# Products that nobody reads on TensorE ahead of three layer norms of a four-layer graph network

## What is computed

```python
xn = _layernorm(x, axis=-1)
x = x + gnn(xn, edge_index, ...) + mix(xn[None], ...)[0]
x = x + ffn(_layernorm(x, axis=-1)[None], ...)[0]
```

```python
def _layernorm(x, axis=-1, eps=1e-05):
    m = jnp.mean(x, axis=axis, keepdims=True)
    v = jnp.var(x, axis=axis, keepdims=True)
    return (x - m) / jnp.sqrt(v + eps)
```

## Time and profile before

| what | us |
|---|---|
| median of 3 runs | 7233.67 |
| lowest and highest run | 7231.20, 7253.52 |
| the profiled execution | 7236.89 |
| its span, first to last instruction | 7235.2 |
| TensorE busy | 5270.6 (73%) |
| VectorE busy | 4311.6 (60%) |
| GpSimd busy | 3786.5 (52%) |
| mean granted clock of TensorE | 0.825 |

### The profile page before, as it was taken

How to read it: one execution, slowest core, us unless ns; L and a number is a source line. 1 busy time by engine, 2 the same in 40 slices (tenths; PEclk the granted TensorE clock), 3 DMA queues, 4 the chain that set the end, 5 groups by cost and what they waited for, 6 DMA issues and landing times. The chain is left out here.

```text
span 7235.2 us, 73313 instructions
## 1 busy us (share of the span) xinstructions
PE 5270.6 (73%) x20758; PEld 3340.7 (46%) x20758; DVE 4311.6 (60%) x12546; ACT 938.7 (13%) x2436; POOL 3786.5 (52%) x3736
## 2 busy tenths in 40 slices
PE   4451767729767778868787885867778888886798
PEld 3241733327634333347685542544443224334687
DVE  8961977772355555552499887766634774445311
ACT  1010011112200010022201231211010001000222
POOL 2776077705477557715303774037744774774233
PEclk9975789759898865669898997888889998565899
DMA  2110543427633333337542334023335774333565
GB/s 62 49 33 12 174 109 105 105 68 189 152 104 105 82 89 105 106 66 191 149 152 64 103 101 100 9 71 100 102 68 147 210 209 116 105 106 68 183 190 172
DMA packets 345016, 801.97 MB, mean 111 GB/s; under 512 B 96963, under 2 KB 196807, under 8 KB 331845
## 3 DMA queue, kind: packets, MB, share of 16 engines
q0 software_dynamic: 202752, 491.35, 26.5%
q1 hardware_dynamic: 141872, 305.94, 13.5%
HBM read 722.42 MB, written 77.80 MB: 111 GB/s over the span
## 5 line engine op out<-in xcount | busy, mean ns | idle before, releaser
L2129 PE MATMUL bank<-arena 128*125 128x256 f32 (+3 forms) x5824 | 2545.2, 539 | 855.3 <-DMA arena<-TAB,arena 349.5
L2112 POOL DMA_INDIRECT arena<-TAB,arena x2080 | 1988.3, 956 | 1308.5 <-DMA TAB<-arena 658.0
L2129 PEld LDWEIGHTS bank<-arena 128*125 128x125 f32 x5824 | 1110.3, 230 | 2241.8 <-DVE arena L2152 675.9
L2173 DVE TENSOR_TENSOR arena<-bank,arena 125x256 f32 (+3 forms) x2912 | 1354.3, 465 | 1147.6 <-PE bank L2129 1108.5
L2112 POOL DMA_INDIRECT arena<-TABa,arena x832 | 831.2, 999 | 847.3 <-ACTq L141 575.1
L2152 DVE TENSOR_SCALAR arena<-arena 128x125 f32<-128x125 f32 x2080 | 617.1, 297 | 62.8 <-PE bank L2129 50.9
L1732 POOL DMA_INDIRECT REC<-arena x400 | 449.5, 1124 | 231.0 <-issue 120.4
L1336 POOL DMA_INDIRECT SUM<-arena x192 | 307.4, 1601 | 465.3 <-DVE arena L1546 402.9
L341 PE MATMUL bank<-arena 128*125 128x256 f32 (+4 forms) x1600 | 439.5, 421 | 90.2 <-DVE arena L2268 24.0
L1381 PE MATMUL bank<-arena 128*128 128x256 f32 x2048 | 465.9, 384 | 6.5 <-DVE arena L1534 6.1
L1395 PE MATMUL bank<-arena 128*128 128x256 f32 x2048 | 466.2, 384 | 0.0
(11 more groups left out here) (501 smaller groups left out, 5496.8 us busy)
## 6 DMA issues: line engine op xcount, KB each, us to landing
arena<-L_ffn_pack SPq DMA_DIRECT2D x32, 2054.0 KB, 9.0
arena<-L_ffn_pack SPq DMA_DIRECT2D x64, 1026.0 KB, 5.6
arena<-TAB,arena POOLq DMA_INDIRECT x2080, 2.8
arena<-SLR SPq DMA_DIRECT2D x52, 512.0 KB, 3.7
arena<-DLR SPq DMA_DIRECT2D x52, 512.0 KB, 4.7
arena<-TABa,arena POOLq DMA_INDIRECT x832, 2.8
arena<-L_ffn_b SPq DMA_DIRECT2D x96, 128.0 KB, 5.6
arena<-LROW SPq DMA_DIRECT2D x20, 610.4 KB
```

Of the source, the lines that this page charges most:

```text
L2112: e.indirect_dma_start(out=m.G[k % RING][:, 0:m.width], out_offset=None, in_=m.table[:, :], in_offset=bass.IndirectOffsetOnAxis(ap=eidx[:, ...
L2129: e.matmul(ps[0:P, 0:m.full], m.S[k % SRING], m.G[k % RING], start=True, stop=True).then_inc(*put("pass_p", m.g, "summed", k))
L2173: e.tensor_tensor(o, banks.of(m.g, "added", k)[0:P, 0:m.full], o, ALU.add).then_inc(*put("pass_v", m.g, "added", k))
```

## The change

A new function, `unread_pe`, is called at three places of TensorE's program, each time right ahead of `norm_pe`. It takes a bank, and for each step of a list waits for that step and then issues 28 matrix products of bf16: the first 128 of J128's 256 columns read as bf16 are the stationary operand, all 256 are the moving one. All go to the same 256 columns of one bank, each starting anew, and nothing reads them. At layers 0 and 2 the list is the five adds of the join and then the first half's variance; at layer 3 it is tiles 4, 9, 14, 19 and 24 of the last sum and then the first half's variance. Nothing else changes.

```diff
--- before.py
+++ after.py
@@ -305,6 +305,19 @@
         turn_act(e, g, XT, AFTER)
 
     gateW, gateb = at(PV + 496, 2, 8, p=128), [at(PV + 512 + 8 * i, 8) for i in range(2)]
+
+    def unread_pe(e, g, steps):
+
+
+        v = J128.bitcast(BF16)
+        ps, before = banks.take(g, "unread")
+        if before:
+            e.wait_ge(*of(*before))
+        for step in steps:
+            e.wait_ge(*of(*step))
+            for i in range(28):
+                ins = e.matmul(ps[:, 0:256], v[:, 0:128], v, start=True, stop=True)
+        ins.then_inc(*put("unread_p", g, "unread"))
 
     def norm_pe(e, g, gate=None):
 
@@ -3026,6 +3039,7 @@
         pass_pe(e, gats[0].run, [l0_queries_pe(e)], LOW)
         r = rest(e, r + 1)
         banks.clear()
+        unread_pe(e, "n0f", [("a0", "joined", i) for i in range(5)] + [("n0f", "var", 0)])
         norm_pe(e, "n0f", gate_of(moes[0]))
         r = rest(e, r + 1)
         banks.clear()
@@ -3052,6 +3066,7 @@
         pass_pe(e, gats[1].run, l2_mix_pe(e), LOW3)
         r = rest(e, r + 1)
         banks.clear()
+        unread_pe(e, "n2f", [("a2", "joined", i) for i in range(5)] + [("n2f", "var", 0)])
         norm_pe(e, "n2f", ("f2", f2wr, "half_p", "gate"))
         r = rest(e, r + 1)
         banks.clear()
@@ -3060,6 +3075,7 @@
         r = rest(e, r + 1)
         banks.clear()
         l3_gnn_pe(e)
+        unread_pe(e, "n3f", [("d3", "out", t) for t in range(4, T, 5)] + [("n3f", "var", 0)])
         norm_pe(e, "n3f", gate_of(moes[2]))
         r = rest(e, r + 1)
         banks.clear()
```

## The result

The changed kernel took 7253.48 us, the median of 17 runs (7236.75 to 7436.58), beside 7234.97 for the kernel before in 17 runs; the ratio is 1.0018, with an interval of 1.001 to 1.0026. The 7436.58 is a single run at a mean granted clock of 0.747 instead of some 0.83, and the ratio leaves it out. The forecast was 7228.7 with a range of 7216 to 7246. The loss is smaller than the 0.3% that counts as a measurable change, and it has the sign that only two of the rivals had.

A forecast was written before the change was run, and what follows sets the result against it. Stages between barriers were taken to end in a TensorE chain of some 27 us at half clock. Gains of 2.2 + 1.0 + 1.8 = 5.0 us off the median of 7233.67 gave 7228.7, range 7216 to 7246.

The forecast's parts named there:

- two of the rivals: Cases with a slower sign: nothing or up to 3 us slower (0.22), and backlog at half clock, 41 slower (0.04).
- No other engine, DMA queue or semaphore wait of another engine changes: Step on the whole program: the change only adds 504 products to TensorE's queue, 168 ahead of each of three norms.
- later stages start as cold as before: Step on stages behind the norms: no clock gain carries over, because some 20 us at half clock lie between.
- Price of a product: Added bf16 products of 256 columns: 0.109 us each at full clock, 0.22 at half.
- Rise and hold of the clock: TensorE's clock rises 4 us after dense work starts and holds 3.6 to 5.0 us after it ends.
- Layer 0: Norm at layer 0: transposes delayed but hidden, first gate product unmoved, part of the gate chain at full clock; gain 2.2 us.
- Layer 2: Norm at layer 2: same shape, mostly at full clock already; loss of 0.3 to gain of 3.1 us, taken as 1.0.
- Layer 3: Norm at layer 3: backlog makes the first gate product 1.0 us late, but the clock holds longer; net gain 1.8 us.
- The clock holds through the chain: Rival: full clock lasts through the gate products that end the three stages; 27 us faster, 7206.7; chance 0.08.
- The unread products don't raise the clock: Rival: products at half clock back up ahead of the gate products at all three norms; 41 us slower, 7274.8; chance 0.04.
- The Trainium skill, "TensorE: Matmul & The Clock Gate", Part 4: Rule against the forecast: transposes don't count for the clock as products do, so it drops before gate products; 2.9 us slower.
- The range: Whole kernel: forecast's own 7223.6 to 7233 us, widened by nothing, small losses and the runs' spread to 7216 to 7246.

The follow-up runs named there:

- e7: The changed kernel run again, all 504 products added to the kernel before; ratio 1.0017 to the kernel before.
- e5: The kernel before with one more semaphore allocated and no instruction more; ratio 0.9996 to the kernel before.
- e6: The whole change, all 504 products, but counted on the old semaphore of the transposes; ratio 1.0022 to the kernel before.
- e8: The kernel before with the 168 products ahead of layer 3's norm alone, on the old semaphore; ratio 1.0005 to the kernel before.
- e15: The kernel before with one more unused buffer of 64512 bytes in DRAM, declared ahead of the others; ratio 0.9998 to the kernel before.
- e1: The kernel before, unchanged, run again; ratio 1.0005 to the kernel before.
- e18: The kernel before with 896 products left out of TensorE's last expert stage; ratio 0.982 to the kernel before.
- e17: The kernel before with 2016 one-column copies added on ScalarE in layer 3's stage; ratio 1.0004 to the kernel before.
- e13: The kernel before with 504 products of 8 columns at the very end of TensorE's program; ratio 1.0015 to the kernel before.
- e4: The changed kernel with all 504 products narrowed from 256 columns to 8; ratio 1.0019 to the kernel before.
- e16: The kernel before with 1512 products of 8 columns at the very end of TensorE's program; ratio 1.0067 to the kernel before.

## Why the prediction was wrong

The step that failed is the sentence "No other engine, DMA queue or semaphore wait of another engine changes", and with it "later stages start as cold as before": it took the three stages as all that can move. The term missing from the sum is layer 0's expert stage, 14.3 us in the traces, 15.3 between e7 and e5 on one chip (275.0 against 259.7). What the runs showed in its place is that adding instructions to TensorE's program slows the weights' transfers of that stage (202 to 214 ns a packet) and that TensorE waits longer for rows; why stays open. Less 2.7 it leaves 11.6, or 0.0016 of 7235, and the ratio is 1.0018.

Point by point:

- *Price of a product:* forecast 0.109 at full clock. 28 took 3.24 us, 0.116 each with the last one's drain; they start 0.110 apart. Right.
- *Rise and hold of the clock:* forecast 4 us for the rise; it was 5.3 at layer 0, 5.0 at layer 2 and 5.3 at layer 3, and 2.7 to 5.8 over the other traces. At layer 0 it held to 1562.95, within the 1562.7 to 1566 of the text.
- *Layer 0:* the first gate product was unmoved (32.37 us behind the first add, before 32.38), the transposes took 1.93 and hid as said. Gain 1.7 for 2.2: right. e7 and e6 have 57.4 and 59.4 us here for 60.2.
- *Layer 2:* gain 0.5 for 1.0. The first gate batch took 2.05 us instead of 2.53; the kernel before had most of this already, as the text said. One execution says little here: e7 and e6 have 57.3 us, e5 and e8 60.0 and 60.2, so by the means of three traces with the change and three without the gain is 2.0.
- *Layer 3:* gain 0.5 for 1.8. Mechanism right, size off. The products took 21.13 us for 20.4, because the clock rose 5.3 us after the first of them and not 4, the transposes 1.87 for 1.7, and the first gate product came 1.9 us late, not 1.0. The lateness also went a way that the working left out: VectorE's first copy waited 1.44 us for it, VectorE works in order, and so the second half's statistics, its tiles and chunk 2's transposes came later, too:

```profile
6692.40 0.68 DVE L284 COPY arena<-bank 128x500 f32<-128x500 f32 x1 [1.44 <-PE bank L271]
...
6696.55 0.90 DVE L234 BATCH_NORM_AGGREGATE arena<-arena 125x2 f32<-125x6 f32 x12
```

```profile
6693.56 1.88 PE L339 MATMUL bank<-arena 128*125 128x8 f32 x16
...
6696.18 1.81 PE L339 MATMUL bank<-arena 128*125 128x8 f32 x16
...
6699.06 1.41 PE L271 MATMUL bank<-arena 125*128 125x125 f32 x7 [0.91 <-ACT arena L257]
6700.26 3.38 PE L339 MATMUL bank<-arena 128*125 128x8 f32 x16
```

  Two batches of gate products ran at full clock, up to 6700.0, as forecast, and TensorE then stood 0.91 us for tiles. e7 and e6 have 50.2 and 49.5 us, e5 49.9. So the three norms by the means of these traces gave 1.8 + 2.0 + 0.2, 4.0 us of the 5.0 forecast.
- *The rivals.* "The clock holds through the chain" fell: 0.50 from 1566 to 1588 with TensorE busy for 21.04 of 22 us. "The unread products don't raise the clock" fell by its mechanism, although the time came out on its side. The Trainium skill, "TensorE: Matmul & The Clock Gate", Part 4, would have the clock down before the gate products, as the prediction read it; they began at full clock in all three stages. At layer 0 that was 4.3 us after the last product, less than the 5.0 us of hold in the earlier trace rows, so this alone decides nothing; what speaks against the page is the rise behind transposes alone in the earlier trace rows. The trace calls these transposes MATMUL and does not tell whether they run in the mode that the page means.
- *The range.* A gain of 2 to 10 us below 7233.67 is 7223.7 to 7231.7, not 7223.6 to 7233. It took the spread of three runs for all that isn't the mechanism. e15's stage of 269.6 us against e1's 253.3 shows that such a stage moves by 16 us with no instruction changed, and the text did not look for stages without slack.

## What to carry to other kernels

Before a gain of a few microseconds is promised, look for stages whose loop has no slack against its transfers: here gathers issued a microsecond later against a weight load went with waits of 4 us each, and the stage lost about four times what the norms gained (15.5 us, the mean of after, e7 and e6 less that of before and e5, against 4.0). Unrolled instructions were not free here even where an idle engine ran them; test that by putting the same number behind the end of the program, where they can delay nothing. Treat one interval that leaves out 1 by 0.0003 as a question: twice the dose answered it. And where a stage's length wanders, look for a quantity that wanders less, such as the time of a packet.

## What was unexpected in the hardware

- With 1512 products that run in the last 45 us, a stage 6 ms earlier was 291.2 us long instead of 258.9. The packets of queue q8 follow the length of TensorE's program: 179 before, 183 with 504 products, 191 with 1512, 173 with 896 fewer in e18, and still 179 with ScalarE's 2016 copies in e17; one packet (16 KB by 2.93 MB over 179) for 126 products or so.
- Products of 8 columns with a weight load each start 0.028 us apart in e13, back to back, and the granted clock was 0.50 from 7949 to 7954 with TensorE busy for 4.78 of these 5 us; in e4 the norm at layer 0 was no shorter by them. Those of 256 columns were at full clock 5.3 us after the first. The gate products of the earlier trace rows kept TensorE busy for 27.66 of 28 us at 0.50, too.
- A gap of 4 us is followed by some microseconds below full clock in the midst of dense fp32 products (0.60 from 1708.3 to 1712.0), so that such a wait costs TensorE twice. The mean clock of the stage is 0.97 in before, 0.95 in after and 0.93 in e16, with 4, 6 and 8 waits for rows.
